# Delta-rule layers of a hybrid conv and attention model: one tile per turn of the loop, a state step per tile, solution steps as 32x32 blocks

## The chip, the cores and the metric

The kernel runs on one core of one Trainium2 chip, as one launch. The core has TensorE (PE for its matrix products, PEld for its weight loads), VectorE (DVE), ScalarE (ACT), GpSimd (POOL) and SyncE (SP, which only issues transfers here). Each engine works through its own instructions in order and meets the others through semaphores. The metric is the device time in microseconds, the median of several runs.

## What is computed

A feature map of 4 images, 256 channels and 32x32 positions goes through seven layers (a convolution block with a gate, a halo attention, two delta-rule layers with a dense layer between them, a pattern layer with top-k steps, an attention with mixed heads, and an expert layer). The change touches the two delta-rule layers alone. In them each of the 1024 positions of an image is one step of a recurrence, and the images are independent:

```python
def delta_rule(q, k, v, beta):
    def step(W, inp):
        qt, kt, vt, bt = inp
        wk = jnp.einsum('bhde,bhe->bhd', W, kt)
        v_new = bt * (vt - wk)
        W = W + jnp.einsum('bhd,bhe->bhde', v_new, kt)
        out = jnp.einsum('bhde,bhe->bhd', W, qt)
        return (W, out)
    W0 = jnp.zeros((bsz, H, D, D), dtype=q.dtype)       # H = 8 heads, D = 32
    _, outs = jax.lax.scan(step, W0, (q, k, v, beta))
    return outs

def fast_ff(x, ln_g, ln_b, slow_w, out_w):
    h = layer_norm(x, ln_g, ln_b)
    qkvb = jnp.einsum('sbi,oi->sbo', h, slow_w).reshape(slen, bsz, H, 3 * D + 1)
    q, k, v, beta = jnp.split(qkvb, [D, 2 * D, 3 * D], axis=-1)
    q, k, beta = jax.nn.softmax(q), jax.nn.softmax(k), jax.nn.sigmoid(beta)
    attn = delta_rule(q, k, v, beta)
    return x + jnp.einsum('sbd,od->sbo', attn.reshape(slen, bsz, H * D), out_w)
```

All arithmetic is in 32-bit floats.

## The kernel before

`fast_weight_stage` runs once for each of the two layers (its tiles are named fw...). It does not walk the 1024 steps one by one. The 4096 tokens lie in 32 tiles of 128 tokens, a tile being 128 neighbouring positions of one image, and a tile in four chunks of 32 tokens. For every chunk and head the 32 steps are solved as a triangular system of 32x32, and only between chunks the state M of 32x32 per head is carried.

The body of the loop works on three tiles at once, each in another phase. For tile i+1 it projects (L669, `project`), takes softmaxes on DVE, and transposes q, k and beta times k (L679 to L681, `turn`). For tile i it forms the products of keys and queries within each chunk (L691, `gram`), masks them on DVE (`lower`, `causal`), and builds the inverse of the triangular system from five rounds of 32x32 products (L698, `product`), in two factors. The factors are spread on ACT into block-diagonal matrices of 128x128 (L838, `spread`: z3x and ntx). For tile i-1 it applies them to the right sides: `solve` at L704, eight products of 128x128 weights by 64 columns, four times per tile. For tile i-2 it goes through the four chunks one after another: `through_state` (L715), the subtraction `corrected` on DVE (L952), `with_state` (L723, L728), the addition to the state on DVE (L957); then `inside` (L736) adds what the tokens of the tile give each other, and ACT copies the result into H (L883). At a new image DVE sets the state to zero by a multiplication (L988).

Since three tiles are under way, kk, tr and intra have four buffers each, and rhs, pu and pkt two. Buffers are chosen when the program is built, so the loop body holds four tiles: `bodies` writes five bodies out, runs a loop of six turns of four tiles (L625), and writes six more out. All waits between engines are written out by hand, and each engine's order is the order of its `body` function. On PE the steps of the phases take turns, so that one phase's products cover another's evictions.

Every 32-bit matmul of the source stands in the program of PE as four instructions (two weight loads and two products), a transposition as two. With the waits and register steps a tile is some 1274 instructions and a turn of the loop 5094, counted in the program as built. The longest other loops on PE are the two of the head-mixing stage: an inner one of 748 instructions (L1822) inside an outer one of 2487 (L1718).

Of the kernel before, what the change touches and what calls it, by code (L numbers as in the profile page):

```python
# [580 lines left out]
def fast_weight_stage(k, layer, H):  # L581
# [4 lines left out]

    nc, d = k.nc, k.d
    n_ = f"fw{layer}"
    HG = 4
    QKN = 2 * C  # L590
    with ExitStack() as ctx:
# [5 lines left out]
        q = sb("q", [P, C]); kk = sb("kk", [P, 4, C])  # L597
# [4 lines left out]
        l8, l8t, bg, loff, qm, z1, z2, tt, z3, l2 = (  # L602
            compact(n) for n in "l8 l8t bg loff qm z1 z2 tt z3 l2".split())
        z3x, ntx = (sb(n, [P, HEADS, P]) for n in ("z3x", "ntx"))
        r0, rk = sb("r0", [P, HEADS, 2, DH]), sb("rk", [P, HEADS, 2, DH])
        pu = sb("pu", [P, 2, C]); pk = sb("pk", [P, C]); pkt = sb("pkt", [P, 2, C])
        U = sb("U", [P, C])
        intra = sb("intra", [P, 4, HEADS, P])
        keep = sb("keep", [P, NT])
        M = sb("M", [P, 2, P])  # L610
        names = ("w zero staged proj dif exp qk tr trc ga gb bg l8 qm lo in t l2 tt z nt zx y r0 ap rk pu pt ptc "
                 "ra u rm m intra fin go dch").split()
        (s_w, s_zero, s_staged, s_proj, s_dif, s_exp, s_qk, s_tr, s_trc, s_ga, s_gb, s_bg, s_l8, s_qm, s_lo, s_in,
         s_t, s_l2, s_tt, s_z, s_nt, s_zx, s_y, s_r0, s_ap, s_rk, s_pu, s_pt, s_ptc,
         s_ra, s_u, s_rm, s_m, s_intra, s_fin, s_go, s_dch) = (k.sem(f"s_{n_}_{n}") for n in names)
        bank = k.bank
        TPI = HW // TILE
        rows = lambda c: slice(32 * c, 32 * c + 32)
        flat = lambda ap: ap.rearrange("p h j -> p (h j)")

        def bodies(body, eng, start=None):
# [10 lines left out]
            for i in range(NT - 4, NT + 2):  # L632
                body(i, i % 4, i + 1 < NT, i < NT, i - 1 < NT, True)
# [4 lines left out]
        with nc.Block() as block:  # L638
            @block.sync
            def _(sp):  # L640
                sp.dma_start(w[:, :, :], d[f"slow{layer}"]).then_inc(s_w, 16)

            @block.gpsimd
            def _(pool):
                off = k.const("off")[:, 0:DH].unsqueeze(1).broadcast_to([P, HEADS, DH])

                def body(i, a, nxt, ch, so, rc):
                    if nxt:
                        pool.wait_ge(s_proj, i + 2)
                        pool.tensor_copy(stage[:, :, :], H[:, :, bass.ds((i + 1) * TILE, TILE)]).then_inc(s_staged, 1)  # L650
                    if ch:
                        pool.wait_ge(s_bg, i + 1)
                        if since(i, 1):
                            pool.wait_ge(s_t, i * 5)
                        pool.tensor_tensor(loff[:, :, :], bg[:, :, :], off, ALU.mult).then_inc(s_lo, 1)  # L655

                for to in (z3x, ntx):
                    pool.memset(to[:, :, :], 0.0).then_inc(s_zero, 1)
                for a in range(4):
                    pool.memset(intra[:, a, :, :], 0.0).then_inc(s_zero, 1)  # L660
                bodies(body, pool)

            @block.tensor
            def _(pe):
                def project(i):
                    pe.wait_ge(s_staged, i + 1)
                    for b, (lo, hi) in ((0, (0, QKN)), (1, (QKN, 3 * C + HEADS))):
                        for h in range(CH):
                            mm = pe.matmul(bank[b][:, 0:hi - lo], stage[:, h, :], w[:, h, lo:hi],  # L669
                                           start=(h == 0), stop=(h == CH - 1))  # L670
                    mm.then_inc(s_proj, 1)

                def turn(i, a):
                    pe.wait_ge(s_qk, i + 1)
                    if since(i, 2):
                        pe.wait_ge(s_ptc, i - 1)
                    for c in range(2):
                        to = slice(P * c, P * c + P)
                        pe.transpose(bank[3][:, P * c:P * c + P], q[:, to], k.const("ident"))  # L679
                        pe.transpose(bank[3][:, C + P * c:C + P * c + P], kk[:, a, to], k.const("ident"))  # L680
                        mm = pe.transpose(bank[4][:, to], rhs[:, a % 2, 1, to], k.const("ident"))  # L681
                    mm.then_inc(s_tr, 1)

                def gram(a, half, sig):

                    for g in range(2):
                        for c in range(4):
                            for jb in range(2):
                                j = 2 * half + jb
                                at = 96 * (2 * g + half)  # L690
                                mm = pe.matmul(bank[jb][rows(c), at:at + 96], tr[rows(j), a, 2, g, rows(c)],  # L691
                                               tr[rows(j), a, :, g, rows(c)], start=True, stop=True)
# [9 lines left out]
                def solve(by, of, sig):  # L702
                    for n in range(HEADS):
                        mm = pe.matmul(bank[2][:, 64 * n:64 * n + 64], by[:, n, :], of(n), start=True, stop=True)  # L704
                    mm.then_inc(sig, 1)

                def turn_keys():
                    for g in range(2):
                        mm = pe.transpose(bank[4][:, C + P * g:C + P * g + P], pk[:, P * g:P * g + P], k.const("ident"))
                    mm.then_inc(s_pt, 1)  # L710

                def through_state(a, c):
                    for g in range(2):
                        at = slice(P * g + 32 * c, P * g + 32 * c + 32)
                        mm = pe.matmul(bank[6][rows(c), P * g:P * g + P], pkt[:, a % 2, at], M[:, g, :],  # L715
                                       start=True, stop=True)
                    mm.then_inc(s_ra, 1)

                def with_state(a, c):

                    for g in range(2):
                        for j in range(4):
                            pe.matmul(bank[7][rows(j), P * g + 32 * c:P * g + 32 * c + 32], M[rows(j), g, rows(j)],  # L723
                                      tr[rows(j), a, 1, g, rows(c)], start=(c == 0 and g == 0), stop=False)
                    for g in range(2):
                        for j in range(4):
                            at = P * g + 32 * j
                            mm = pe.matmul(bank[6][rows(j), C + at:C + at + 32], kk[rows(c), a, at:at + 32],  # L728
                                           U[rows(c), at:at + 32], start=True, stop=True)
                    mm.then_inc(s_rm, 1)  # L730

                def inside(a):
                    for g in range(2):
                        for j in range(HG):
                            hd = HG * g + j
# [1787 lines left out]
```

## Time and profile before

| what | us |
|---|---|
| median of three runs | 5330.31 |
| lowest and highest | 5323.69, 5341.91 |
| profiled execution, span (no other time of it is listed) | 5373.4 |
| first delta-rule stage, from its weights' transfer at 331.5 to its last copy into H | 908.5 |
| second one, 1614.3 to 2467.4 | 853.1 |
| the 24 tiles of the first stage's loop, 443 to 1119 | 676 |

The page gives busy time by engine, then 40 slices of the span, the queues of the DMA engines, the chain that ended last, and groups of instructions. In the delta-rule stages PE is the busiest engine by far. PEclk is the share of TensorE's clock that was granted: 1.0 is 2.4 GHz and 0.5 is 1.2 GHz, and the clock stands at one of the two at any time. A queue of the kind "instruction" carries the engines' own programs into the core. "issue" behind a row is idle time in which the engine waited for nothing that the profile shows.

### The profile page before, as it was taken

The numbers are of one execution on the slowest core, as the hardware profiler recorded it, in microseconds if no ns is written. First come the engines' busy times: TensorE is split into PE (matmuls) and PEld (weight loads), VectorE is DVE, ScalarE is ACT, GpSimd is POOL, SyncE is SP. The second block draws the span as 40 slices with busy tenths as digits, with TensorE's granted clock in tenths as the row PEclk, the third lists the DMA queues.
The fourth block names the chain that finished last, engine by engine and source line by source line (L and its number), as shares of the span: only waits on it lengthen the run. The fifth ranks groups of instructions, "written<-read, shape, count | busy, mean of one in ns | idle before, by whom it ended". The sixth has DMA issues, their size and how long they took to land. (4 is left out here: it accounts for less than half of the span.)

```text
span 5373.4 us, 139944 instructions
## 1 busy us (share of the span) xinstructions
PE 4530.5 (84%) x57100; PEld 2834.8 (53%) x57101; DVE 2972.1 (55%) x5849; ACT 2152.0 (40%) x4091; POOL 831.7 (15%) x2139
## 2 busy tenths in 40 slices
PE   3679898887997888897688886799999999984995
PEld 1237777773436777774355554354454545433663
DVE  3444444453024544454488886488686877852343
ACT  1133223232123333331466664277575766721221
POOL 0000000000000000000355553011111111104012
PEclk7788878798998988898899998899999999985997
DMA  1000000000000000000100000000000000006123
GB/s 42 2 7 3 3 3 3 3 3 18 0 0 9 4 3 3 3 4 3 38 1 1 1 1 0 10 1 1 1 0 1 0 1 1 0 3 217 61 84 101
DMA packets 47552, 85.70 MB, mean 16 GB/s; under 512 B 7121, under 2 KB 38129, under 8 KB 46065
## 3 DMA queue, kind: packets, MB, share of 16 engines
q1 hardware_dynamic: 40944, 61.84, 3.3%
q0 software_dynamic: 6144, 16.79, 1.0%
q8 instruction: 401, 6.57, 0.5%
q14 instruction: 63, 0.51, 0.0%
HBM read 45.05 MB, written 33.55 MB: 15 GB/s over the span
## 5 line engine op out<-in xcount | busy, mean ns | idle before, releaser
L1775 PE MATMUL psum<-hm_ex,hm_mix 128*128 128x512 f32 x1024 | 510.4, 621 | 42.3 <-ACT hm_Aq L1855 38.3
L1841 ACT ACTIVATE hm_ex<-psum,hm_nm 128x1024 f32<-128x1024 f32 x256 | 285.6, 1116 | 299.4 <-DVE hm_nm L1899 299.4
L1775 PEld LDWEIGHTS psum<-hm_ex,hm_mix 128*128 128x128 f32 x1024 | 175.6, 191 | 352.5 <-issue 344.8
L1914 DVE COPY hm_A<-psum 128x1024 f32<-128x1024 f32 x256 | 312.9, 1222 | 51.5 <-PE psum L1784 47.9
L1909 DVE TENSOR_SCALAR_CACHE_REDUCE hm_plus<-hm_Aq,hm_cbcol,hm_sums 128x1024 f32<-128x1024 f32 x256 | 340.5, 1330 | 0.0
L1899 DVE TENSOR_REDUCE hm_nm<-psum 128x1 f32<-128x1024 f32 x256 | 311.0, 1215 | 13.5 <-PE psum L1763 13.5
L1784 PEld LDWEIGHTS psum<-K,hm_Aq 128*128 128x128 f32 x2048 | 236.6, 140 | 150.0 <-issue 145.4
L957 DVE TENSOR_TENSOR fw_M<-fw_M,psum 128x256 f32<-128x256 f32 x256 | 107.8, 421 | 348.1 <-PE psum L728 345.6
L1846 ACT ACTIVATE hm_junk<-hm_Aq 128x1024 f32<-128x1024 f32 x256 | 270.6, 1057 | 30.3
L1763 PE MATMUL psum<-hm_kt,hm_qd 64*32 64x512 f32 x4096 | 280.1, 606 | 0.0
L1321 ACT ACTIVATE pt_signs<-pt_acts,pt_tb 128x1024 f32<-128x1024 f32 (+1 forms) x224 | 227.6, 1018 | 116.1 <-POOL pt_tb L1188 95.0
L1784 PE MATMUL psum<-K,hm_Aq 128*128 128x128 f32 x2048 | 266.6, 273 | 5.7 <-DVE hm_A L1914 5.6
L1855 ACT ACTIVATE hm_Aq<-psum 128x1024 f32<-128x1024 f32 x256 | 259.5, 1014 | 11.1 <-PE psum L1775 11.1
L704 PE MATMUL psum<-fw_rk,fw_ntx 128*128 128x64 f32 x2048 | 253.9, 278 | 0.0
L704 PEld LDWEIGHTS psum<-fw_rk,fw_ntx 128*128 128x128 f32 x2048 | 247.4, 194 | 6.7
L715 PE MATMUL psum<-fw_M,fw_pkt 128*32 128x128 f32 x1024 | 185.2, 310 | 74.3 <-issue 38.1
L669 PE MATMUL psum<-fw_w,fw_stage 128*128 128x512 f32 (+1 forms) x512 | 226.6, 593 | 22.9 <-POOL fw_stage L650 19.0
L655 POOL TENSOR_TENSOR fw_loff<-fw_bg,K 128x256 f32<-128x256 f32 x64 | 57.0, 890 | 1163.2 <-DVEq L937 1163.2
L1235 PE MATMUL psum<-pt_w_proc,pt_keptT 128*128 128x512 f32 x512 | 225.6, 599 | 10.3 <-ACT pt_keptT L1306 10.3
L2226 ACT ACTIVATE ex_ht<-psum,ex_b 128x128 f32<-128x128 f32 x320 | 91.2, 368 | 324.6 <-PE psum L2158 241.6
L1692 POOL TENSOR_TENSOR hm_mix<-hm_kron,hm_rinv 128x128 f32<-128x128 f32 x256 | 102.1, 399 | 664.8 <-DVE hm_rinv L1904 664.8
L1405 DVE TENSOR_SCALAR_CACHE_REDUCE pt_over<-pt_acts,pt_tb 128x1024 f32<-128x1024 f32 (+1 forms) x96 | 101.7, 1097 | 161.9 <-POOL pt_tb L1188 161.9
(379 smaller groups left out, 9044.6 us busy)
## 6 DMA issues: line engine op xcount, KB each, us to landing
ex_rows_in<-ex_zero SPq DMA_DIRECT2D x2, 5120.0 KB, 24.8
ex_xs<-ex_rows_in SPq DMA_DIRECT2D x80, 128.0 KB
ex_rows_out<-ex_ys SPq DMA_DIRECT2D x80, 128.0 KB, 1.7
ex_w<-in_ex_w SPq DMA_DIRECT2D x2, 4096.0 KB
X<-in_x SPq DMA_DIRECT2D x2, 2048.0 KB, 12.5
out_y<-X SPq DMA_DIRECT2D x2, 2048.0 KB, 9.0
ff_w<-in_ff_w SPq DMA_DIRECT2D x2, 1024.0 KB, 5.8
pt_w_proc<-in_pt_proc SPq DMA_DIRECT2D x1, 2048.0 KB, 7.6
```

The lines of the kernel that those rows point to most:

```text
L669: mm = pe.matmul(bank[b][:, 0:hi - lo], stage[:, h, :], w[:, h, lo:hi], start=(h == 0), stop=(h == CH - 1))
L704: mm = pe.matmul(bank[2][:, 64 * n:64 * n + 64], by[:, n, :], of(n), start=True, stop=True)
L1321: act.activation(signs[:, u, 0:n], acts[:, lane(j), u, 0:n], ACT.Sign, bias=tb[:, lane(j), u, 0:1], accum_out=tb[:, lane(j), u, 1:2]).then ...
L1763: mm = pe.matmul(bank[2 * u + c][32 * pr:32 * pr + 32, :], qd[64 * c:64 * c + 64, u, pr, :, :].rearrange("p j n -> p (j n)"), kt[64 * c:64 ...
L1775: mm = pe.matmul(bank[4 + c], mix[:, u, :], ex[:, u, 512 * c:512 * c + 512], start=True, stop=True)
L1784: mm = pe.transpose(bank[6 + m // 4][:, P * (m % 4):P * (m % 4) + P], Aq[:, u, P * m:P * m + P], k.const("ident"))
L1841: act.activation(ex[:, u, :], flat2(psum[:, 2 * u:2 * u + 2, :]), ACT.Exp, bias=nm[:, u:u + 1], accum_out=rsum[:, u:u + 1]).then_inc(s_ex, 1)
L1846: act.activation(junk[:, :], Aq[:, u, :], ACT.Square, accum_out=ssq[:, bass.ds(b * TI + i, 1)]).then_inc(s_sq, 1)
L1855: act.activation(Aq[:, u, :], flat2(psum[:, 4:6, :]), ACT.Copy).then_inc(s_cp, 1)
L1899: dve.tensor_reduce(nm[:, u:u + 1], flat2(psum[:, 2 * u:2 * u + 2, :]), AX.X, ALU.max, negate=True).then_inc(s_nm, 1)
L1909: dve.tensor_scalar(plus[:, :], Aq[:, u, :], cbcol[:, :], sums[:, :], ALU.add, ALU.add, accum_out=sums[:, :]).then_inc(s_run, 1)
L1914: dve.tensor_copy(A[:, :, :, QT_ * t:QT_ * t + QT_], flat2(psum[:, 6:8, :]).rearrange("p (m g n) -> p m g n", m=MT, g=HEADS)).then_inc(s_a ...
```

## The change

A tile is now 32 positions of each of the four images, so that its four chunks are four independent recurrences: the state M holds all images, and there is one state step per tile instead of four. `through_state` becomes 2 halves of 16 small products (L763), `corrected` and `state` one DVE operation each, `read_state` (L745) reads the output of the state and `new_state` (L774) forms its increment. There is no multiplication of the state by `keep`.

The body has four phases (new, inv, sol, rec) and one tile per turn: the loop runs over tiles 4 to 31, four bodies stand ahead of it and three behind it. All tiles have one buffer. What has to live longer goes elsewhere: rhs is copied into `held` by ACT, and kk, the transposed queries and the masked products qm are written by SP to a tensor in DRAM (`away`), and read back as `late` two tiles later. The factors stay compact: `solve` is now 32 products of 32x32 weights by 64 columns (L730), and the spreads into z3x and ntx are gone.

```diff
-        rhs = sb("rhs", [P, 2, 2, C])
-        tr = sb("tr", [P, 4, 3, 2, TILE])
+        rhs = sb("rhs", [P, 2, C]); held = sb("held", [P, 2, C])
+        tr = sb("tr", [P, 3, 2, TILE])
-        z3x, ntx = (sb(n, [P, HEADS, P]) for n in ("z3x", "ntx"))
+        late = sb("late", [P, 3, C])
+        away = nc.dram_tensor(f"{n_}_away", (NT, P, 3, C), F32).ap()
...
-            for i in range(-1, 4):
-                body(i, i % 4, i + 1 < NT, i >= 0, i >= 1, i >= 2)
-            with eng.Fori(1, NT // 4 - 1) as j:
+            for i in range(4):
+                body(i, True, i >= 1, i >= 2, i >= 3)
+            with eng.Fori(4, NT) as i:
                 if start:
                     start()
-                for a in range(4):
-                    body(j * 4 + a, a, True, True, True, True)
+                body(i, True, True, True, True)
...
+                def body(i, new, inv, sol, rec):
+                    v, s = i - 1, i - 2
+                    if inv:
+                        sp.wait_ge(s_qm, v + 1)
+                        sp.dma_start(there(v, 2), qm[:, :, :].rearrange("p h j -> p (h j)")).then_inc(s_om, 16)
+                    if new:
+                        sp.wait_ge(s_qk, i + 1)
+                        sp.dma_start(there(i, 0), kk[:, :]).then_inc(s_okk, 16)
+                        sp.wait_ge(s_trc, i + 1)
+                        sp.dma_start(there(i, 1), tr[:, 1, :, :].rearrange("p g t -> p (g t)")).then_inc(s_oq, 16)
+                    if sol:
...
+                        sp.dma_start(late[:, :, :], away[bass.ds(s, 1), :, :, :].rearrange("o p n c -> p (o n) c")
+                                     ).then_inc(s_late, 16)
...
                 def solve(by, of, sig):
                     for n in range(HEADS):
-                        mm = pe.matmul(bank[2][:, 64 * n:64 * n + 64], by[:, n, :], of(n), start=True, stop=True)
+                        for b in range(4):
+                            mm = pe.matmul(bank[2][rows(b), 64 * n:64 * n + 64], by[rows(b), n, :], of(n)[rows(b)],
+                                           start=True, stop=True)
...
+                def softmax(i):
                     if since(i, 1):
                         dve.wait_ge(s_tr, i)
+                        dve.wait_ge(s_okk, i * 16)
+                        dve.wait_ge(s_hold, i)
...
+                def state(r):
+                    dve.wait_ge(s_ui, r * 2 + 2)
+                    whole = M[:, :, :, :, :].rearrange("p b s g e -> p b (s g e)")
+                    dve.tensor_tensor(whole, whole, psum[:, 6:8, 128:256], ALU.add).then_inc(s_m, 1)
```

On PE, the end of the loop's body. Before, this is the end of the fourth tile of a turn:

```order
L681 MATMUL psum<-K,fw_rhs 128x128
L824 REGISTER_ALU
L723 MATMUL psum<-fw_tr,fw_M 32x32 x8
L728 MATMUL psum<-fw_U,fw_kk 32x32 x8
L736 MATMUL psum<-fw_intra,fw_U 32x128 x8
L625 REGISTER_ALU
L625 COMPARE_AND_BRANCH
```

Now it is the end of every tile in the loop:

```order
L736 MATMUL psum<-K,fw_pk 128x128 x2
L859 REGISTER_ALU
L723 MATMUL psum<-fw_z,fw_loff 32x32 x32
L716 MATMUL psum<-fw_tr 32x96 x16
L730 MATMUL psum<-fw_held,fw_z 32x64 x32
L716 MATMUL psum<-fw_tr 32x96 x16
L628 REGISTER_ALU
L628 COMPARE_AND_BRANCH
```

The jump back, which came once in four tiles, comes once per tile; a turn is 1760 instructions instead of 5094, and a tile 1760 instead of 1274.

On PE, the middle of a tile, where solution steps (fw_ntx or fw_nt with fw_rk) alternate with products (fw_z, fw_l) and state steps. Before:

```order
L704 MATMUL psum<-fw_rk,fw_ntx 128x64 x8
L698 MATMUL psum<-fw_z,fw_l 32x32 x32
L793 REGISTER_ALU
L715 MATMUL psum<-fw_M,fw_pkt 32x128 x2
L796 ISA
L698 MATMUL psum<-fw_z,fw_l 32x32 x32
L800 REGISTER_ALU
L723 MATMUL psum<-fw_tr,fw_M 32x32 x8
L728 MATMUL psum<-fw_U,fw_kk 32x32 x8
```

Now:

```order
L730 MATMUL psum<-fw_rk,fw_nt 32x64 x32
L825 ISA
L745 MATMUL psum<-fw_late,fw_M 32x32 x32
L754 MATMUL psum<-fw_intra,fw_U 32x128 x8
L832 ISA
L723 MATMUL psum<-fw_z,fw_l 32x32 x32
L836 REGISTER_ALU
L730 MATMUL psum<-fw_rk,fw_nt 32x64 x32
L774 MATMUL psum<-fw_U,fw_late 32x32 x16
```

A solution step went from 8 matmuls to 32, and the four rounds of L715, L723 and L728 became one round of L763, L745 and L774.

On SP, whose queue held nothing within the loop before, the rows of one turn now:

```order
L650 DMA fw_away<-fw_qm 128x256
L652 REGISTER_ALU
L653 ISA
L653 DMA fw_away<-fw_kk 128x256
L655 ISA
L655 DMA fw_away<-fw_tr 128x256
L658 ISA
L659 ISA
L662 ISA
L662 DMA fw_late<-fw_away 128x768
```

Three writes of 128 KB and a read of 384 KB per tile came in.

## Rows read from the trace of the kernel before

**Rows 1.** The page's head

```profile
span 5373.4 us, 139944 instructions
```

**Rows 2.** Busy time by stretch: both stages, a tile after a jump, a tile, head-mixing

```profile
core 0: us, PE busy (x) PEld busy (x) DVE busy (x) ACT busy (x) POOL busy (x), PEclk, DMA share, GB/s
331.00:1239.60 908.60, 792.24 (x19968) 643.48 (x19968) 422.30 (x1060) 267.08 (x674) 46.49 (x70) 0.83 0.02 4
1602.00:2471.00 869.00, 751.82 (x19976) 610.72 (x19976) 429.14 (x1069) 273.46 (x685) 46.50 (x70) 0.87 0.02 4
1920.00:1950.00 30.00, 26.81 (x615) 21.97 (x615) 12.81 (x32) 7.64 (x20) 1.34 (x2) 0.72 0.01 3
1950.94:1974.44 23.50, 21.03 (x625) 17.27 (x624) 13.15 (x33) 7.79 (x20) 1.34 (x2) 1.00 0.02 3
3541.00:3716.00 175.00, 169.60 (x1752) 88.20 (x1744) 152.07 (x209) 129.82 (x201) 33.71 (x79) 1.00 0.00 0
```

**Rows 3.** PE in order of time, 1896 to 1929: start us, us, instruction, idle before

```profile
1896.19 0.30 PE L736 MATMUL psum<-fw_intra,fw_U 128*32 128x128 f32 x1 [1.11 <-issue]
...
1899.59 0.56 PE L691 MATMUL psum<-fw_tr 32*32 32x96 f32 x32
...
1905.44 2.87 PE L669 MATMUL psum<-fw_w,fw_stage 128*128 128x512 f32 x8
1908.14 1.89 PE L704 MATMUL psum<-fw_rk,fw_ntx 128*128 128x64 f32 x16
1909.97 0.75 PE L698 MATMUL psum<-fw_z,fw_l 32*32 32x32 f32 x64
1910.65 0.62 PE L715 MATMUL psum<-fw_M,fw_pkt 128*32 128x128 f32 x4
...
1922.23 1.05 PE L715 MATMUL psum<-fw_M,fw_pkt 128*32 128x128 f32 x4 [3.45 <-issue]
1923.22 3.68 PE L704 MATMUL psum<-fw_rhs,fw_z3x 128*128 128x64 f32 x16
```

**Rows 4.** Jumps of PE, by line: ns min/median/max, first and last start

```profile
L625 PEldq COMPARE_BRANCH  x12: 83/3743/3971, 551.0 to 2345.8; - x12
...
L1822 PEldq COMPARE_BRANCH  x24: 76/215/239, 3540.3 to 4697.6; - x24
...
L1718 PEldq COMPARE_BRANCH  x4: 78/3420/3850, 3758.0 to 4741.0; - x4
```

**Rows 5.** Instruction packets from 1950.9 to 1974.4, one tile: packets, MB, share

```profile
q8 instruction: 5, 0.08, 1.6%
```

**Rows 6.** All packets from 3541 to 3716, five turns of L1822's loop

```profile
DMA packets 0, 0.00 MB, mean 0 GB/s; under 512 B 0, under 2 KB 0, under 8 KB 0
```

**Rows 7.** Instruction packets from 3758 to 4084, one turn of L1718's loop

```profile
q8 instruction: 11, 0.18, 0.2%
```

**Rows 8.** Transfers in 40 slices of 0.25 us, 549 to 559, around a jump

```profile
GB/s 0 0 0 0 0 0 0 0 0 0 0 0 0 0 66 0 0 0 0 0 0 0 0 0 0 0 66 0 0 0 0 0 0 0 0 0 0 0 0 0
```

**Rows 9.** The same for 664 to 674, around the next jump

```profile
GB/s 0 0 0 0 0 0 0 0 66 0 0 0 0 0 0 0 0 0 0 0 0 0 66 0 0 0 0 0 0 0 0 0 0 0 0 0 0 0 0 0
```

**Rows 10.** DVE in order of time, a chunk's state steps from 810 on

```profile
810.89 0.35 DVE L988 TENSOR_SCALAR fw_M<-fw_M,fw_keep 128x256 f32<-128x256 f32 x1 [1.61 <-PE psum L736]
811.96 0.41 DVE L952 TENSOR_TENSOR fw_U<-fw_pu,psum 32x256 f32<-32x256 f32 x1 [0.72 <-PE psum L715]
814.74 0.42 DVE L957 TENSOR_TENSOR fw_M<-fw_M,psum 128x256 f32<-128x256 f32 x1 [2.37 <-PE psum L728]
```

**Rows 11.** ACT in order of time, the two spreads of a tile's factors

```profile
807.30 1.68 ACT L838 ACTIVATE fw_z3x<-fw_z 32x256 f32<-32x256 f32 x4
809.00 1.53 ACT L838 ACTIVATE fw_ntx<-psum 32x256 f32<-32x256 f32 x4
```

**Rows 12.** SP's transfers: count, size each, median us to landing

```profile
ex_rows_out<-ex_ys SPq DMA_DIRECT2D x80, 128.0 KB, 1.7
...
fw_w<-in_slow SPq DMA_DIRECT2D x2, 776.0 KB, 4.5
```

More of the change, by code:

```diff
@@ L613, in fast_weight_stage @@
[L613 to L617, printed above, removed]
+        l8, l8t, bg, loff, z1, z2, tt, z3, l2 = (compact(n) for n in "l8 l8t bg loff z1 z2 tt z3 l2".split())
+        qm = sb("qm", [P, HEADS, DH])
@@ L657, in _, with fetch, body @@
[L657 to L661, printed above, removed]
+                def fetch(i):
+                    pool.tensor_copy(stage[:, :, :].rearrange("p h (b n) -> p h b n", b=B), tokens(i)).then_inc(s_staged, 1)
+                def body(i, new, inv, sol, rec):
+                    if inv:
+                        pool.wait_ge(s_bg, i)
+                        if since(i, 2):
+                            pool.wait_ge(s_t, i * 5 - 5)
+                        pool.tensor_tensor(loff[:, :, :], bg[:, :, :], off, ALU.mult).then_inc(s_lo, 1)
+                    if new:
+                        pool.wait_ge(s_pj1, i + 1)
+                        fetch(i + 1)
@@ L663, in _ @@
+                fetch(0)
+                pool.memset(intra[:, :, :], 0.0).then_inc(s_zero, 1)
+                for i in range(4):
+                    body(i, True, i >= 1, i >= 2, i >= 3)
+                with pool.Fori(4, NT - 1) as i:
+                    body(i, True, True, True, True)
+                for i in (NT - 1, NT):
+                    body(i, False, True, True, True)
             @block.tensor
             def _(pe):
[L665 to L676, printed above, removed]
+                def project(i, n, lo, hi, sig):
+                    for h in range(CH):
+                        mm = pe.matmul(bank[n][:, 0:hi - lo], stage[:, h, :], w[:, h, lo:hi],
+                                       start=(h == 0), stop=(h == CH - 1))
+                    mm.then_inc(sig, 1)
+                def turn():
                     for c in range(2):
@@ L708, in turn_keys @@
                     for g in range(2):
-                        mm = pe.transpose(bank[4][:, C + P * g:C + P * g + P], pk[:, P * g:P * g + P], k.const("ident"))
+                        mm = pe.transpose(bank[2][:, P * g:P * g + P], pk[:, P * g:P * g + P], k.const("ident"))
                     mm.then_inc(s_pt, 1)
[L712 to L717, printed above, removed]
@@ new lines, in through_state, with new_state @@
+                    mm.then_inc(s_ra, 1)
+                def new_state(half):
+                    for c in (2 * half, 2 * half + 1):
+                        for g in range(2):
+                            for j in range(4):
+                                at = 64 * half + 32 * g
+                                mm = pe.matmul(bank[6 + c % 2][rows(j), 128 + at:160 + at],
+                                               late[rows(c), 0, P * g + 32 * j:P * g + 32 * j + 32],
+                                               U[rows(c), place(g, j), :], start=True, stop=True)
+                    mm.then_inc(s_ui, 1)
@@ new lines, in body @@
+                    if new:
+                        pe.wait_ge(s_qk, i + 1)
+                        if since(i, 1):
+                            pe.wait_ge(s_qm, i)
+                        turn()
+                    if sol:
+                        pe.wait_ge(s_pu, s + 1)
+                        turn_keys()
+                    if inv:
+                        pe.wait_ge(s_z, v * 2 + 2)
+                        pe.wait_ge(s_lo, v + 1)
+                        pe.sem_inc(s_go, 1)
+                        product(z3, loff)
```

453 lines of the change are left out of this document (216 added, 237 removed).

## The prediction, made before the changed kernel was run

> **What bounds the kernel now.** I read the stages first: the two delta-rule stages take 908.5 and 853.1 us, a third of the span [rows 1, 2]. Only they change, so the sum is made there, against the profiled span of 5373.4 us, and the difference is put on the median of 5330.31 us (the profile is 0.8% above it; a difference of 80 us changes by less than 1 us through that). Within a stage I compare the engines: in an undisturbed tile of 23.5 us PE has a product in flight for 21.0 us, DVE works 13.2 and ACT 7.8 [rows 2]. So PE sets the pace, and a saving on DVE or ACT counts only where PE waits for it.
>
> Then I ask why 24 tiles of the first loop take 676 us, 28.2 each, where a good tile takes 23.5. PE in order of time answers: 1.11 us idle in the middle of L736 and 3.45 us at the head of a turn, both "issue", so no engine was late [rows 3]. The 3.45 us stand right behind the jump back to the head of the loop, which takes PE's sequencer 3.74 us in the median of twelve [rows 4]. And the stretch behind such a jump runs partly at the clock's lower level: 30 us at a granted 0.72 where a good tile has 1.00, with L704 at 3.68 us instead of 1.89 [rows 2, 3]. What is late is the program itself. A tile brings five instruction packets for 1249 recorded weight loads and products [rows 2, 5], 250 per packet or 256 with the waits: the loop's 5094 instructions come in anew, 16 KB at a time, in every turn. On the page L1822's loop is the counterexample: 748 instructions, a jump of 0.215 us [rows 4], and not one packet in 175 us, five turns [rows 6]. L1718's loop, 2487 instructions, is again of the first kind: 3.42 us per jump, 11 packets per turn [rows 4, 7]. So a loop on PE is either held or brought in again, and this change moves one loop from 5094 to 1760, between the two known cases.
>
> **The change part by part.**
>
> *Solution steps.* Four per tile at 1.89 us become 32 products of 32x32 by 64 columns. A product round (32 matmuls, 32 columns) holds PE from 1909.97 to 1910.65, 0.68 us; two gram halves (32 matmuls, 96 columns) take at most 2 x 0.56 = 1.12 [rows 3]. Issue, not columns, seems to set these, so I take 0.75: 4 x 1.14 = 4.6 us less on PE per tile (bounds 3.1 and 4.8).
>
> *State.* Four rounds of L715 (0.62 each) and of L723 with L728 (16 small matmuls, half a product round, 0.34) are 3.8 us. Now L763, L745 and L774 are 96 small matmuls, three product rounds, 2.0. PE saves 1.8 more: 21.0 - 4.6 - 1.8 = **14.6 us** of PE work per tile at the full clock. At the lower level L715 takes 1.05 for 0.62 and L704 3.68 for 1.89 [rows 3], 1.7 to 1.95 times; small matmuls are nearer to the first, so some 25 us.
>
> *DVE and ACT.* DVE loses L988 and three each of L952 and L957: 0.35 + 3 x 0.41 + 3 x 0.42 = 2.8 us [rows 10], leaving 10.3. With them goes a chain: between L952 and L957 DVE waited 2.37 us for PE, four times a tile. ACT loses the spreads, 1.68 + 1.53 [rows 11], and gets two copies of about 0.5 (nt, held): about 5.6. Both stay below any turn that I find, so beyond the chain this is worth nothing of its own.
>
> *DRAM.* SP now issues three writes of 128 KB and a read of 384 KB per tile. The row for 128 KB is 1.7 us, the next size above 384 KB has 4.5 [rows 12], so a write and a read are 3.4 to 6.2 us. The read is issued in one turn and used in the next, and what waits for a write (softmax on DVE, behind it the solution, z3 and state steps; the next qm; the copies into tr on ACT, behind them pkt, the output and r0) comes most of a turn later. I cost it at nothing under a turn of 14 us or more; without that cover it would be up to 6 us a tile. Single buffers add waits of PE on DVE (s_dif, s_qk, s_qm), each for an operation of the tile before; the same holds.
>
> *Loop body.* A turn is 1760 instructions, 6.9 packets. What I need to know is whether PE holds them. Counting blocks of 256: 748 instructions lie in three or four blocks, and one more is brought ahead; 2487 in ten or eleven, and 11 packets came. So five blocks are held and eleven are not. 1760 lie in eight, unless the loop begins in the first 32 of a block (by the place of the loop in the program it does not), and with the one ahead nine. Nine is two from the case that is not held and four from the one that is; a store that drops the oldest block first holds either the whole circle or none of it, as the 11 packets show, where nothing of the turn before was left. I take **not held**.
>
> Then each tile pays a jump and seven more packets, one after another. Around two jumps the first two packets start 12 and 14 slices of 0.25 us apart, 3.0 and 3.5 us [rows 8, 9]. PE's own work per block is 14.6 / 6.9 = 2.1 us at the full clock, which hides behind a packet except in the projection's blocks and where PE waits: 0.5 to 1. At the lower level it is 25 / 6.9 = 3.6, above a packet: up to 5 per turn. The turn: 3.7 + 7 x 3.0 + 0.5 = 25.2 at best, 3.7 + 7 x 3.5 + 5 = 33 at worst. With idle stretches in every tile I expect the lower level more often than before, and take 3.7 + 7 x 3.2 + 2.9 = **29 us**.
>
> The seven bodies outside the loop are 7007 instructions, 27.4 packets by 3.2 = 88 us, with some 20 us for set-up and drain (estimated): 110. A stage is 28 x 29 + 110 = 922 us against a mean of 880.8; both, +82 us. **Forecast 5330 + 82 = 5412 us**, with 5245 at a turn of 26 and 5580 at 32. At 27.5 us a turn nothing is gained or lost.
>
> The Trainium skill has a rule here that reads the other way: "Runtime: NRT & Kernel Launch", section Instruction fetch mechanics, gives PE a store of 128 KiB, 2048 instructions, refilled in blocks of 16 KiB, and warns that a taken branch outside the window stalls on a fetch. By its bare count 1760 instructions fit, and the sum would be that of the first rival; by its blocks nine of 16 KiB are 144 KiB and do not fit. The trace agrees on the block of 256 instructions and on the stall; no row shows the size of the store.
>
> **The rivals.**
>
> *The turn is held* (the other side: faster). Place: the jump at L628. It decides if PE keeps nine blocks or more, or does not count the one ahead. Then the jump is 0.2 us, no packets come in the loop, and PE's work is the pace: 14.6 us at the full clock, 25 at the lower level, say 19 in the middle, since 14.6 us of work with waits between leaves the clock in doubt. Stage 28 x 19 + 110 = 642, twice 239 less: **4850 us** (4630 at 15, 5180 at 25). For it: a 748-instruction loop is held without a packet [rows 6]. Against: the eleven of L1718.
>
> *Only the blocks that overlap come in again.* If the block ahead pushes out just the loop's first one, a turn costs the jump, 3.7, and one packet, and the rest runs as in the rival above: 15 to 25 plus 4 to 6, about 24. Stage 782, twice 99 less: **5130 us** (4950 to 5370). Against it: L1718's loop, which by this would have kept some of its blocks, brought all 11.
>
> *The change doesn't do what it says*: fewer state steps, but PE waits for the DRAM path. That would need 6 us in the open per tile, 28 x 2 x 6 = 336 us, on a turn of 19: about 5190. The cover of a whole turn speaks against it.
>
> **How the numbers follow.** Not held 0.66, held 0.24, partly 0.08, DRAM path 0.02. The likeliest is 5412 with its own range 5250 to 5550, which holds some nine tenths of that case: 0.60. To leave no more than 0.2 out, the range goes down through the partial case (0.08 with the DRAM path's 0.02) into the upper half of the held one: **4780 to 5550**. A difference of 0.3% (16 us) is about what a measurement of this kernel can tell from none. Slower by more than that needs a turn over 27.8, four fifths of the first case: 0.53. Within it: 0.07. Faster: held 0.24, the partial ones 0.09, and what is left of the first case 0.07, together 0.40.
>
> **What would show it.** In the profile after: if I am right, L628's jumps have a median near 3.7 us in both stages, there are some eight packets per 29 us on the instruction queue, PE's idle time is "issue", and the granted clock of the stages is below 0.83. If the turn is held, the jumps are near 0.2 us, the loop has no packets, and a tile is 15 to 25 us. Solution steps of 0.7 to 0.8 us at the full clock show that term right either way, DVE rows of 0.42 for L957's successor once per tile the other. If jumps are short and the tile still is above 25 us, my reading of the program's arrival as the bound is wrong, and the waits on PE will say for whom it waits.

## The result, and the profile after

The changed kernel takes 5479.1 us (median of four runs, 5477.5 to 5479.9) against 5336.1 of the kernel before: a ratio of 1.0268, 95% interval 1.0252 to 1.0283. It is slower by 143 us where 82 were forecast. The page's head and its instruction queues:

```profile
span 5476.4 us, 171848 instructions
...
q8 instruction: 504, 8.26, 0.7%
q14 instruction: 53, 0.43, 0.0%
```

The two stages, from the weights' transfer to the last copy into H, then one turn of the first stage's loop and two neighbouring turns of the second's. Columns as in [rows 2]:

```profile
core 0: us, PE busy (x) PEld busy (x) DVE busy (x) ACT busy (x) POOL busy (x), PEclk, DMA share, GB/s
329.40:1390.80 1061.40, 678.58 (x27648) 521.43 (x27648) 324.24 (x833) 198.90 (x482) 42.27 (x65) 0.68 0.10 29
1765.60:2605.70 840.10, 620.89 (x27648) 477.94 (x27648) 324.58 (x833) 197.62 (x482) 42.32 (x65) 0.75 0.11 34
1045.20:1079.60 34.40, 21.82 (x879) 16.52 (x866) 10.09 (x26) 6.16 (x16) 1.33 (x2) 0.65 0.09 27
2029.30:2046.50 17.20, 16.54 (x895) 12.89 (x874) 10.10 (x26) 6.07 (x16) 1.33 (x2) 0.90 0.07 23
2046.50:2079.90 33.40, 22.80 (x868) 17.56 (x864) 10.16 (x26) 6.17 (x16) 1.33 (x2) 0.64 0.13 40
```

The first stage went from 908.5 to 1061.4 us, the second from 853.1 to 840.1: together 140 us more, the difference of the medians within 3 us. (The two profiled executions differ by only 103 us, since that of the kernel before spent 2906 us behind its second stage and this one 2871, with the same code there.) Less work is done in both. PE's busy time in the first went from 792 to 679 us [rows 2], although it counts at a lower clock now; what grew is the time in which PE has nothing in flight.

The two stages run the same code, and yet the second has turns of 17 and of 33 us by turns. The jumps back, by line as in [rows 4], in the first stage and in the second:

```profile
L628 PEldq COMPARE_BRANCH  x28: 83/4550/5130, 442.6 to 1345.8; - x28
...
L628 PEldq COMPARE_BRANCH  x28: 76/227/6062, 1874.4 to 2561.0; - x28
```

The last of 28 doesn't jump (76 to 83 ns). In the first stage every other one takes about 4.55 us, and the mean turn is (1345.8 - 442.6) / 27 = 33.45 us. In the second one 14 take about 0.22 us and 13 about 5.7, in strict alternation; the mean is 25.43 us. The instruction packets follow the jumps. In the turn from 1045.2, in the long one from 2046.5 and in the short one from 2029.3 the queues carried:

```profile
q8 instruction: 9, 0.15, 2.0%
```

```profile
q8 instruction: 9, 0.15, 2.0%
```

```profile
DMA packets 433, 0.39 MB, mean 23 GB/s; under 512 B 49, under 2 KB 433, under 8 KB 433
...
q1 hardware_dynamic: 433, 0.39, 6.6%
```

Nine packets in a long turn, none in a short one: all 433 packets there are the tile's own transfers. PE in order of time, a turn of the first stage, shows what the nine cost:

```profile
1084.72 0.47 PE L763 MATMUL psum<-fw_M,fw_pkt 32*32 32x32 f32 x32 [4.61 <-issue]
1085.07 0.64 PE L730 MATMUL psum<-fw_r,fw_nt 32*32 32x64 f32 x15
1087.35 1.54 PE L730 MATMUL psum<-fw_r,fw_nt 32*32 32x64 f32 x49 [1.64 <-issue]
...
1097.37 0.58 PE L730 MATMUL psum<-fw_rk,fw_nt 32*32 32x64 f32 x27 [1.45 <-issue]
...
1101.16 0.86 PE L723 MATMUL psum<-fw_z,fw_l 32*32 32x32 f32 x47 [1.41 <-issue]
...
1104.95 0.42 PE L774 MATMUL psum<-fw_U,fw_late 32*32 32x32 f32 x14 [1.03 <-issue]
...
1112.98 0.75 PE L730 MATMUL psum<-fw_held,fw_z 32*32 32x64 f32 x19 [1.18 <-issue]
```

Every pause shown is "issue", none is a wait for an engine, and three of them follow one another at 3.79 us (1097.37, 1101.16, 1104.95): work of about 2 us, then a stop. The stops come in the midst of a solution step, a product or a state step, and in every turn at the same instructions. Behind the jump PE does 64 instructions of L763, 16 weight loads and 15 products of L730 and 6 waits and steps, then stops: the 101st instruction closes a block. The following stops lie 256 or 512 further on. In the second stage the first stop is at the 156th. So the first loop starts 155 instructions into a block of 256 and the second 100, the 1760 instructions lie in eight blocks both times, and the eighth holds 123 of them in the first stage, 68 in the second. That is the one difference between the stages that I find in the trace, and the experiments start from it.

### The profile page after: what moved, and what is told of

It is laid out like the page before. It is cut to its first block and busy times, and to the rows that moved or that the text cites. A ratio compares the mean times of both kernels' runs of the same rounds, so it can differ in the third digit from the quotient of the medians.

```text
span 5476.4 us, 171848 instructions
## 1 busy us (share of the span) xinstructions
PE 4291.4 (78%) x72460; PEld 2582.9 (47%) x72461; DVE 2775.7 (51%) x5395; ACT 2014.5 (37%) x3707; POOL 823.5 (15%) x2129
## 5 line engine op out<-in xcount | busy, mean ns | idle before, releaser
L697 PE MATMUL psum<-fw_w,fw_stage 128*128 128x512 f32 (+1 forms) x512 | 297.5, 719 | 16.8 <-DMA fw_w<-in_slow 16.8
L892 ACT ACTIVATE fw_l<-psum 128x256 f32<-128x256 f32 x64 | 24.5, 383 | 638.4 <-PE psum L723 638.4
L1013 DVE TENSOR_TENSOR fw_rk<-psum,fw_r 128x512 f32<-128x512 f32 x128 | 88.5, 691 | 310.1 <-PE psum L730 304.5
L983 DVE TENSOR_TENSOR fw_bg<-psum,fw_eb 128x128 f32<-128x128 f32 x128 | 36.6, 286 | 386.6 <-PE psum L716 386.6
L763 PE MATMUL psum<-fw_M,fw_pkt 32*32 32x32 f32 x4096 | 56.9, 218 | 210.3 <-issue 207.7
L730 PE MATMUL psum<-fw_rk,fw_nt 32*32 32x64 f32 x8192 | 174.4, 234 | 50.3 <-issue 48.2
```

The source lines that it names most:

```text
L697: mm = pe.matmul(bank[n][:, 0:hi - lo], stage[:, h, :], w[:, h, lo:hi], start=(h == 0), stop=(h == CH - 1))
```

## Experiments: the place of the loop

Where no interval stands beside a time, it is that of a single run (`thin`: the median of four).

**Only the place is moved.** `aligned` adds steps of an otherwise unused semaphore ahead of the loops, nothing else:

```diff
...
+                for _ in range((118, 54)[layer]):
+                    pe.sem_inc(s_pad, 1)
                 pe.wait_ge(s_w, 16)
                 bodies(body, pe)
```

> The changed kernel with nothing altered but the place of its loop in PE's program: 118 semaphore steps ahead of the first delta-rule stage's loop and 54 ahead of the second's. In the changed kernel PE stalls at instruction 101 of the loop's body in the first stage and at 156 in the second, then every 256, so the loops begin 155 and 100 instructions into a block of 256 and reach into an eighth block; with the steps both begin 16 or 17 into a block and end inside the seventh. Theory A (PE keeps eight blocks, the one it brings ahead among them; seven and one fit, eight and one don't): every jump takes about 0.2 us, no packet comes within the loops, each turn is the short one that the second stage already shows, 17.2 us, and the time is 5479 - 28 x (33.5 - 17.2) - 28 x (25.6 - 17.2) = about 4790 us (4730 to 4830). Theory B (1760 instructions are too many wherever they stand, and the short turns of the second stage have another cause): no change, 5465 to 5495.

Measured: 4746.3 us, a ratio of 0.8905 to the kernel before (0.8869 to 0.8941). The jumps of the two stages (the line is one further down), and a stretch of 19 turns on the queues:

```profile
L629 PEldq COMPARE_BRANCH  x28: 76/208/232, 453.0 to 872.2; - x28
...
L629 PEldq COMPARE_BRANCH  x28: 76/208/221, 1410.6 to 1829.9; - x28
```

```profile
DMA packets 11223, 15.44 MB, mean 51 GB/s; under 512 B 1248, under 2 KB 8672, under 8 KB 11223
...
q1 hardware_dynamic: 11223, 15.44, 16.2%
```

No jump is long, no instruction packet comes between 500 and 800 us, and a turn takes (872.2 - 453.0) / 27 = 15.53 us. That is less than the short turn of the second stage, since the clock now stays up:

```profile
330.10:918.70 588.60, 503.90 (x27648) 404.28 (x27648) 322.11 (x833) 192.28 (x482) 42.40 (x65) 0.92 0.14 45
...
500.00:515.52 15.52, 14.80 (x864) 12.07 (x864) 10.01 (x26) 5.93 (x16) 1.33 (x2) 1.00 0.17 51
```

So 172 instructions more, in no loop, take 733 us away from the changed kernel. Theory B has fallen.

**The two places exchanged.** `swapped` is the same edit with (201, 110).

> The changed kernel with 201 semaphore steps ahead of the first stage's loop and 110 ahead of the second's: the first loop then begins 100 instructions into a block, where the second one stood, and the second 155 into a block, where the first one stood. Theory A: the two stages change places: the first one alternates between turns of about 17 and 34 us (jumps 0.2 and 5.6 us by turns), the second has 34 us in every turn and a jump near 4.5; the sum stays at 5479 (5460 to 5500). Theory B (the short turns belong to the second stage, whatever the place): the first stage keeps 33.5 us a turn and the second its alternation.

```profile
L629 PEldq COMPARE_BRANCH  x28: 76/232/5917, 464.5 to 1152.8; - x28
...
L629 PEldq COMPARE_BRANCH  x28: 79/4577/5133, 1696.3 to 2605.3; - x28
```

The first stage now alternates (13 long jumps, a mean turn of 25.5 us) and the second is long throughout (33.7): the place decides, not the stage. The time, 5521 us, is above the expected range, by what the 311 steps cost: in `aligned` 118 of them start between 330.2 and 348.1 us, 0.15 each, so these take 48 us, of which only the wait for the weights hides a part (PE's first product of the first stage starts at 361.28 us here and at 334.31 in the changed kernel).

**Start of the loop or number of blocks?** Both kernels would also agree with a rule on where the jump's target lies in its block. `longer` keeps the starts of `aligned` (with the filling of `aligned_mm`, below) and makes the loop longer by 192 instructions: `gram(1, ...)` runs four times over, with the same result.

> The kernel aligned_mm, in which each turn of the two loops repeats the last half of the key and query products three times more (48 products of 32x32 by 96, 192 instructions, the same result): the loops still begin 16 or 17 instructions into a block, but have 1952 instructions and reach 177 into an eighth block. Theory A (eight blocks, the one ahead among them): what counts is the number of blocks that a turn touches, so both loops are brought in again in every turn, jumps near 4.5 us, nine packets, 34 to 35 us a turn: 4729 + 56 x 19 = about 5790 us (5700 to 5850). Rival I (what counts is where the target of the jump lies in its block, and the aligned kernel is fast because the target is near a block's start): jumps stay at 0.2 us, a turn is 15.5 + 3 x 0.6 = 17.3 us and the time about 4830.

```profile
L629 PEldq COMPARE_BRANCH  x28: 83/4202/4603, 441.8 to 1327.2; - x28
...
L629 PEldq COMPARE_BRANCH  x28: 83/3956/4717, 1863.0 to 2763.5; - x28
```

The packets of the instruction queue from 441.8 to 1327.2, the 27 turns of the first stage:

```profile
q8 instruction: 242, 3.96, 2.1%
```

5681 us, turns of 32.8 and 33.4: the same start, but 177 instructions in an eighth block, and the whole program comes in again in every turn, nine packets each. Rival I has fallen. The turn is a little below the expected 34, and the time therefore below the expected range (5700 to 5850). It is no longer than with 1760 instructions, so the added products cost nothing that shows.

**How far into the eighth block?** In `edge` the loop ends 4 instructions short of the end of the seventh block (first stage) and 16 into the eighth (second); in `edge2` 4 and 32 into the eighth.

> The changed kernel with 129 semaphore steps ahead of the first stage's loop and 75 ahead of the second's, so that the first loop begins 28 instructions into a block and ends with the seventh block but for 4 instructions, and the second begins 48 into a block and has 16 instructions in an eighth. Theory A (eight blocks, the one ahead among them): first stage held in every turn, 15.5 us, no packets. For the second stage A has two forms. A1, the block ahead is asked for as soon as the sequencer enters the last block: bringing in the ninth costs the first one its place, and turns are long (34 us) or alternate as with 68 instructions in the eighth block. A2, it is asked for a while later, so that with only 16 instructions left the jump comes first: held in every turn. The time is 4750 with A2, 4990 with alternating turns, 5250 with long ones. Against A altogether: packets in the first stage's loop.

> The changed kernel with its loops 36 and 64 instructions into a block (34 and 20 dead products and 1 and 3 semaphore steps ahead of them, the second stage's counted from where the first one's leave it), so that 4 and 32 instructions lie in an eighth block. In the edge kernel, with 16, two turns were long and 25 short; in the changed kernel, with 68, long and short turns alternate. If the block ahead is asked for a fixed while after the sequencer enters the last block, the first stage (4 instructions) is held in every turn but perhaps the first two, and the second (32) has some long turns, fewer than 14. If it is asked for at once, both stages alternate as with 68. Time between 4730 (no long turn) and 5250 (both alternate).

The second stage of `edge`, and the first and second of `edge2`:

```profile
L629 PEldq COMPARE_BRANCH  x28: 83/215/5687, 1415.3 to 1875.5; - x28
```

```profile
L629 PEldq COMPARE_BRANCH  x28: 76/208/216, 439.5 to 861.2; - x28
...
L629 PEldq COMPARE_BRANCH  x28: 76/228/5906, 1394.4 to 2079.3; - x28
```

| instructions in the eighth block | stage | jumps over 1 us, of 27 |
|---|---|---|
| none | both of `aligned`, first of `edge` | 0 |
| 4 | first of `edge2` | 0 |
| 16 | second of `edge` | 2, among the first four |
| 32 | second of `edge2` | 13 |
| 68 | second of the changed kernel, first of `swapped` | 13 |
| 123 | first of the changed kernel, second of `swapped` | 27 |
| 177 | both of `longer` | 27 |

`edge` took 4794 us, `edge2` 4997. What follows: seven blocks and the one brought ahead stay on PE, eight and one do not. The middle rows need one thing more. If the block ahead is asked for only some while after PE's sequencer has entered the last one, a loop that leaves that block at once never asks for the ninth, and eight blocks stay; with more instructions there a turn sometimes asks and loses everything. This is A2 in the main, but A2 as I had put it allowed no long turn at 16 instructions, and I had expected fewer long turns with 32 than with 68. The runs don't show when the request goes out, nor why 32 and 68 instructions give strict alternation rather than a mixture. Two packets start together at the head of a long turn (in `edge` at 1435.0 and 1435.3 us); which blocks they are is not shown.

## Experiments: what a long turn is made of

**Jump or packets?** `four` gives PE's loop four tiles per turn, so that a jump comes once in four tiles, as before the change, while every tile still brings its 1760 instructions:

```diff
-                bodies(body, pe)
+                for i in range(4):
+                    body(i, True, i >= 1, i >= 2, i >= 3)
+                with pe.Fori(1, NT // 4) as j:
+                    for a in range(4):
+                        body(j * 4 + a, True, True, True, True)
+                for i in range(NT, NT + 3):
+                    body(i, False, i < NT + 1, i < NT + 2, True)
```

> The changed kernel with four tiles per turn of PE's loop (7045 instructions, one jump in four tiles, as before the change; the other engines keep one tile per turn). No tile can be held now, in either stage. Theory E (the jump is the loss): a tile is 33.5 - 3/4 x 4.6 = 30 us. Theory F (the serial packets are, 6.9 per tile at about 3.8 us, which PE's own 14.8 us of work cannot fill): 6.9 x 3.8 + 1.2 for a quarter of a jump + 1 to 2 for the projection's blocks = 28 to 29 us. Either way the first stage gains about 28 x 4, the second, which had 25.6, loses about 28 x 3.5: 5440 to 5490. A tile near 20 us would say that jumps alone made the loss.

```profile
L881 PEldq COMPARE_BRANCH  x7: 83/3308/3383, 526.1 to 1224.9; - x7
...
L881 PEldq COMPARE_BRANCH  x7: 83/3562/3921, 1841.2 to 2554.9; - x7
```

5473 us. A tile takes (1224.9 - 526.1) / 24 = 29.1 us in the first stage and 29.7 in the second. E's 30 and F's 28 to 29 lie too near each other for this run to choose; it prices both. Three quarters of a jump are worth 33.45 - 29.1 = 4.3 us, so a jump with what follows from it is 5.8. (Packets fall too, from nine a tile to 7.25, 174 in the 24 tiles.) Of the 17.9 us that a long turn has over a held one (33.45 - 15.53) the other 12.1 are then packets that come one after another. By this reckoning jumps made up a third of the loss.

**Do the tile's transfers slow the packets, or pace the turn?** In `thin` each of the four transfers moves the first partition alone, so that most of what is read back is left out of the computation; `aligned_thin` is the same with the loops held:

```diff
...
-                        sp.dma_start(there(i, 0), kk[:, :]).then_inc(s_okk, 16)
+                        sp.dma_start(there(i, 0)[0:1], kk[0:1, :]).then_inc(s_okk, 16)
...
```

> The changed kernel with its four transfers per tile cut to the first partition (1 KB writes, a 3 KB read; the rest of what is read back stays zero, so that part of the computation is left out). Theory C (the tile's DRAM transfers slow the instruction packets): jumps fall from 4.5 to about 3.7 us and the spacing of packets from 3.8 to about 3.2, a turn that brings its program in falls by some 4 us, and the time by 42 x 4 = 170, to about 5310. Theory D (the packets take their time by themselves, and the transfers are hidden, as the prediction has it): 5479 within 20 us, spacing unchanged.

> The changed kernel with its loops held (118 and 54 semaphore steps ahead of them) and the four transfers per tile cut to the first partition; what is read back is zero but for that, so part of the computation is left out, and only the two delta-rule stages can be compared, since a later layer's steps depend on the data. Theory G (the DRAM path is covered by the turn, as predicted): a turn stays at 15.5 us within 0.1. Theory H (it paces the held turn: write, write, read in one queue): a turn falls by 1 us or more.

The first stage of `thin`, its second, and the first of `aligned_thin`:

```profile
L628 PEldq COMPARE_BRANCH  x28: 82/4558/5000, 437.2 to 1339.4; - x28
...
L628 PEldq COMPARE_BRANCH  x28: 76/227/5056, 1868.3 to 2541.1; - x28
```

```profile
L629 PEldq COMPARE_BRANCH  x28: 76/208/232, 454.3 to 874.4; - x28
```

A turn of 33.41 us against 33.45, and of 15.56 against 15.53. With next to nothing moved, neither the long turn of the first stage nor the held turn changes: theories D and G. In the second stage C holds for a small part: the longest jump falls from 6.1 to 5.1 us, and the mean turn from 25.43 to 24.92. (The whole times, 9839 and 9131 us, say nothing on this. My expectation of about 5310 or 5479 for `thin` overlooked that the pattern layer has a search that runs only where the data demand it: 1184 steps of it came in on DVE, from 2851 to 7145 us in `aligned_thin` and likewise in `thin`, and in the trace of no other kernel here.)

**The solution steps by themselves.** `wide` goes back to eight products with block-diagonal weights and to the spreads on ACT; its loop has 1377 instructions, in six or seven blocks wherever it starts.

```diff
...
-                        for b in range(4):
-                            mm = pe.matmul(bank[2][rows(b), 64 * n:64 * n + 64], by[rows(b), n, :], of(n)[rows(b)],
-                                           start=True, stop=True)
+                        mm = pe.matmul(bank[2][:, 64 * n:64 * n + 64], by[:, n, :], of(n), start=True, stop=True)
...
```

> The changed kernel with the solution steps of before: eight products with block-diagonal 128x128 weights, the factors spread on ACT (two spreads of 1.5 to 1.7 us per tile come back); nothing is moved otherwise, and the loop's body has 1377 instructions, which lie in six or seven blocks wherever they begin. Theory A: held in both stages, jumps 0.2 us, no packets in the loops; a turn is 17.2 us + four steps at 1.0 us more = 21 to 23, and the time 5479 - 28 x (33.5 - 22) - 28 x (25.6 - 22) = about 5060 (5000 to 5110). Theory B with a bound below 1377: jumps near 4.5 us and packets in every turn, over 5400.

The jumps of the first stage, then one turn and its first solution step by engine (columns as in [rows 2]) and PE in order of time within it:

```profile
L629 PEldq COMPARE_BRANCH  x28: 76/208/221, 445.1 to 1095.1; - x28
```

```profile
642.10:666.00 23.90, 21.68 (x694) 17.83 (x674) 10.15 (x28) 8.99 (x23) 1.33 (x2) 0.86 0.10 33
...
642.17:645.64 3.47, 3.47 (x28) 3.47 (x17) 2.18 (x6) 0.09 (x1) 0.94 (x1) 0.50 0.00 0
```

```profile
642.17 3.67 PE L731 MATMUL psum<-fw_r,fw_ntx 128*128 128x64 f32 x16
645.64 3.15 PE L699 MATMUL psum<-fw_w,fw_stage 128*128 128x512 f32 x4
...
651.51 1.98 PE L731 MATMUL psum<-fw_rk,fw_ntx 128*128 128x64 f32 x16
653.42 0.75 PE L745 MATMUL psum<-fw_late,fw_M 32*32 32x32 f32 x64
...
662.85 2.00 PE L731 MATMUL psum<-fw_held,fw_z3x 128*128 128x64 f32 x16 [1.61 <-ACT fw_z3x L886]
```

Held in both stages, as A has it, and 5198 us, below the kernel before, though the loop was placed by nothing. But a turn is 24.1 us in the first stage, (1095.1 - 445.1) / 27, not 21 to 23, and the time is above the expected 5000 to 5110. Against the held turn of `aligned`, where a step at the full clock is

```profile
531.75 1.10 PE L731 MATMUL psum<-fw_r,fw_nt 32*32 32x64 f32 x64
532.77 1.98 PE L698 MATMUL psum<-fw_w,fw_stage 128*128 128x512 f32 x4
...
537.47 1.09 PE L731 MATMUL psum<-fw_rk,fw_nt 32*32 32x64 f32 x64
538.36 0.78 PE L746 MATMUL psum<-fw_late,fw_M 32*32 32x32 f32 x64
```

three steps cost about 1.0 us more each, the fourth 2.6 (3.67 against 1.10, at a granted clock of 0.50), PE waits 1.61 us for ACT's spread, and the projection runs partly at the lower clock (1.1 more): 8.3 us, and 15.5 + 8.3 = 23.8. My expectation had four steps at 1.0 and no more. So the compact factors are worth more than PE's own time: with them goes a wait, and in a turn without it the granted clock was 1.00, against 0.86 in the turn of `wide`. That the wait is what brings the clock down was not tried by itself.

**A cheaper filling.** `aligned_mm` fills the 118 and 54 places with 29 and 13 dead products and two steps each.

> The aligned kernel with the 118 and 54 places filled by 29 and 13 dead 32x32 products (four instructions each) and two semaphore steps, instead of semaphore steps alone. In the aligned one a step takes 0.15 us, so that PE began the first stage at 348 instead of 334 us; 116 instructions of small products take about 1.5. Both theories of the place: loops held as in aligned, turns of 15.5 us. The time is 4746 - 13 = 4733 us (4725 to 4742).

4729.5 us, 0.8867 (0.8832 to 0.8902) of the kernel before, the fastest kernel here. The steps in `aligned`, PE's first products there, and PE here:

```profile
L880 PEldq EVENT_SEMAPHORE  x118: 51/51/51, 330.2 to 348.1; - x118
```

```profile
348.37 2.05 PE L698 MATMUL psum<-fw_w,fw_stage 128*128 128x512 f32 x2 [21.93 <-issue]
```

```profile
330.00 3.27 PE L882 MATMUL psum<-K 32*32 32x32 f32 x58 [4.04 <-PEq L98]
334.43 4.70 PE L698 MATMUL psum<-fw_w,fw_stage 128*128 128x512 f32 x8 [1.17 <-DMA fw_w<-in_slow]
```

The stage's projection begins at 334.43 instead of 348.37 us, when the weights are there. The gain of 17 us is near the 13 expected, though the two ratios' intervals overlap; in the profiles the stages are 12.0 and 4.3 us shorter.

## Why the prediction was right, and where it was not

The sign, its cause and the range (4780 to 5550) held; the size was 82 us for a measured 143. Point by point:

- **The loop is not held.** Right in the first stage, with the signs that the prediction named: long jumps, "issue" as PE's only idle time, a granted clock below 0.83 (0.68 and 0.75 in the two stages). In the second stage the median jump is 0.23 us, which the prediction had named as the sign of a held turn. The counting was right too, nine blocks with the one ahead where eight stay. But it was a guess between a loop of five blocks and one of eleven, and `aligned` shows how near the edge was.
- **"Holds either the whole circle or none of it".** This is the step that failed, in the second stage. It took the ninth block as asked for in every turn. Where the loop leaves its last block early it isn't always, and then the whole circle stays: 14 turns of about 17.6 us that no case of the prediction had. The rival in which only overlapping blocks come in again would give turns of 24 us in both stages; the second one's mean of 25.43 is not that but two kinds of turn.
- **The price of bringing in.** Mis-sized. The jump took 4.55 us for 3.7. Behind it the prediction had 7 x 3.2 + 2.9 = 25.3 us, and the turn has 33.45 - 4.55 = 28.9. The 3.2 came from the first two packets behind a jump [rows 8, 9]; in a long turn of this kernel they start farther apart. Transfers in 40 slices of 0.25 us, from 1090 to 1100 and from 1100 to 1110 (each 66 is a packet of PE's program, the rest the tile's transfers):

```profile
GB/s 0 0 0 0 0 0 0 0 0 0 0 0 0 0 0 0 0 0 66 0 0 0 0 0 0 0 0 0 0 0 0 0 0 0 0 66 0 0 0 0
...
GB/s 0 0 0 0 37 340 148 0 0 66 0 0 0 0 0 0 0 0 0 0 0 0 0 0 66 0 0 0 0 0 0 0 0 0 0 0 0 0 0 0
```

  The distances are 17, 14 and 15 slices, 3.8 us in the mean. The prediction took the two distances that it had for the usual one.
- **Two errors that nearly cancel.** 33.45 and 25.43 average to 29.4 us a turn, where 29 was forecast, so the forecast turn looks better than its working was. The profile's two stages are 57.5 us above the forecast 2 x 922. Of these 24 are 0.44 us a turn, 56 times; 33 are the seven bodies outside the loop, 1061.4 - 28 x 33.45 = 125 us in the first stage and 128 in the second, for 110. Their 27.4 packets at 3.8 instead of 3.2 us would be 16 us of the 15 and 18; that is an estimate, not shown by itself.
- **PE's work.** 14.6 us forecast, 14.80 measured in a held turn at the full clock. A solution step takes 0.89 us (537.47 to 538.36), not 0.75, still 1.0 below the 1.89 of before [rows 3]. The prediction took the number of products to set a step, not their columns; a product round of 32 columns takes 0.68 [rows 3], this one of 64 columns 0.89, so the columns count too. DVE and ACT were forecast at 10.3 and 5.6 and are at 10.01 and 5.93.
- **The DRAM path at nothing.** Right in a held turn, shown by `aligned_thin` at a turn of 15.56 us, and in the long turns of the first stage, shown by `thin`.
- **The held rival** (4850, between 4630 and 5180) is what `aligned` and `aligned_mm` are. Its mechanism was right with the turn at its lower end; the stage outside the loop is 588.6 - 28 x 15.53 = 154 us there, a first turn that is brought in among them.
- **Two slips in the rivals' sums.** The held rival at a turn of 25 us comes to 5189, not 5180; and 15 to 25 us plus 4 to 6 for the overlapping blocks would be 4850 to 5520, not 4950 to 5370. Neither enters the forecast.

On the Trainium skill, "Runtime: NRT & Kernel Launch", section Instruction fetch mechanics: of its two readings the one by blocks was borne out (eight blocks of 256, a loop with the block ahead in nine doesn't fit), and the bare count of 2048 instructions misleads, as 1760 and 1952 were brought in again. The same section calls the cost of crossing into the next block mostly hidden; in the long turn shown above five of seven crossings stopped PE for 1.0 to 1.6 us.

## What to carry to other kernels

Count a PE loop in blocks of 256 instructions from where it really starts, add one, and stay within eight; then place it, since a hundred instructions ahead of the loop can decide. Many small products instead of few large ones save PE's time only while their instructions stay on the engine: each block that comes in costs about 3.8 us, so a block must hold that much work to hide it. Pauses named "issue" at the same instruction of every turn are the sign, and the instruction queue's packets per turn are the proof.

## What the runs showed of the hardware

- A jump of PE takes 0.21 us to a target that is there and 3.3 to 6.1 us to one that is not (`four` 3.3 to 3.9, first stage of the changed kernel 4.55, alternating stage 5.7).
- Eight blocks of 256 instructions stay on PE, the one brought ahead among them. This is worked out: a loop in seven blocks was held for 27 jumps in a row without a packet, and so was one with 4 instructions in an eighth; with 123 or more there every turn brought in nine packets. With 16 to 68, turns of both kinds follow each other in one loop.
- A semaphore step of PE's queue takes (348.1 - 330.2) / 117 = 0.15 us, 18 us for 118 of them, where 29 dead 32x32 products (116 instructions) take 3.27.
- The granted clock was 1.00 over a held turn of `aligned`, 0.64 and 0.65 over long turns with the same work, and 0.90 over the short turn right behind a long one. In `wide` it was 0.86 over a turn and 0.50 over that turn's first solution step, which took 3.67 us there and 1.10 in the held turn of `aligned`, where the step is made of small products.
